# Attention heads in the order 3, 7, 0, 4, 1, 5, 2, 6, with the q copies split by column half

## The chip, the cores and the metric

The kernel runs on one core of a Trainium2 chip. The metric is the device time of one launch in microseconds (us), lower is better. One launch works through a batch of 8 graphs, one after the other, with the same program for each.

## The reference

Input is `x` (8 x 1024 nodes x 256 features), an adjacency `adj` (8 x 1024 x 1024) and a node mask. Four pre-normed residual layers follow each other; the second is the one that the change touches:

```python
h = jnp.maximum(_layernorm(x, axis=-1), 0.0)
x = x + _L1_gnn_ref(h, adj, adj, Wq, bq, Wk, bk, Wv, bv, Wo, bo, 1024)
# in _L1_gnn_ref: 8 heads of 32 features
q, k, v = (proj(Wq, bq), proj(Wk, bk), proj(Wv, bv))
scores = jnp.einsum('bhqd,bhkd->bhqk', q, k) * SCALE
scores = scores * (adj_matrix + bond_matrix)[:, None, :, :]
attn = jax.nn.softmax(scores, axis=-1)
ctx = jnp.einsum('bhqk,bhkd->bhqd', attn, v)        # heads side by side: 256 features
return jnp.einsum('bse,fe->bsf', ctx, Wo) + bo
```

The order in which heads are taken changes nothing in the result as long as the rows of `Wo` follow it.

## The kernel before

Every engine has its own hand-written instruction stream; counters (semaphores, one `Signal` per step) order them. A batch is a chain of stages: graph layer 0, attention (layer 1), hypergraph convolution (layer 2), dense graph attention (layer 3). Nothing of the next batch's matmul work overlaps the attention of this one, so a delay at the start of the attention moves all that is behind it.

**How q and k reach the score matmuls.** Projection gives q and k transposed, features on the partitions: 2 groups of 4 heads, 32 partitions a head. Each value is split into a rounded part and the rest: `khi`, `klo`, `qhi`, `qlo` (128 partitions x 2 groups x 1024 nodes, 8 KB a partition each). A score matmul contracts over 128 partitions at once, in which the four products hi·hi, hi·lo, lo·hi, lo·lo of one head are stacked: `kS[:, head]` holds khi, khi, klo, klo and `qS[:, head]` holds qhi, qlo, qhi, qlo in its four blocks of 32 partitions. A head has a place j (0 to 3) in its group of four (`HPG`). Places 0, 1 and 2 are brought into the stacks by DMA from the SP queue: for each place 4 copies for kS and 4 for qS, each 32 partitions x 2 groups x 1024 columns (256 KB). These are 24 copies a batch. Place 3 (heads 3 and 7) is stacked by TensorE with `pick` matrices (L940) and moved by ScalarE (L865). `K_DONE` is the count of `lo_s` at which all of k is split; SP starts the kS copies there, all three places, and then the qS copies.

**The attention loop.** A unit u is one head of one tile of 128 queries, 64 units a batch (`UNITS`), 8 heads for each of 8 tiles. For unit u: `scores(u)` on TensorE (2 matmuls, L1056, into PSUM banks 0 to 3 in turn); the mask, scale and row maximum on VectorE (L684, writes `Z`); the exponential on ScalarE (L882); `transposes(u)` on TensorE (8, L1076, three PSUM banks in turn); `evacuate(u)` copies them to `PT`, one half by ScalarE (L874), one by VectorE (L645), every fourth unit both by ScalarE; after four units `weighted_values` (L1097). TensorE issues scores of unit u + 2 ahead of the transposes of unit u.

Two things in this order matter. `scores(0)`, `(1)`, `(2)` each wait for one place of qS, since heads 0, 1 and 2 come first, and the whole loop is behind the wait for all of kS:

```python
pe.wait_ge(*kS_in(b, 64 * (HPG - 1)))
...
if u < HPG - 1:
    pe.wait_ge(*qS_in[u](b, 64))
```

And `PT` lies in the same memory as the sources of the copies (region p1: `khi`, `klo`, `qhi`, `qlo` in one layout, 8 slots of `PT` of 4 KB a partition in the other): slots 0 to 3 lie over khi and klo, slots 4 to 7 over qhi and qlo. Before, the waits of TensorE cover this, as every copy has landed before the evacuation of unit 0, 1 or 2 can begin.

`keep_warm` are matmuls without use (L962) that keep TensorE busy.

Of the kernel before, what the change touches and what calls it, by code (L numbers as in the profile page):

```python
# [5 lines left out]
F32 = mybir.dt.float32  # L6
# [8 lines left out]
LOWEST = -3.0e38  # L15
TINY = 1.2e-38


# [11 lines left out]
def build_program(nc, x_in, adj_in, mask_in, wqkT0, wv0, w1attn, bq1, bk1, bv1, bo1,  # L30
# [4 lines left out]
    NH = N // HALF  # L35
# [9 lines left out]
    PTS = 8  # L45
    ZS = 3
    SCORE_SCALE = 2.0 * float(HD) ** -0.5
    W_SCALE = 1.0 / float(D) ** 0.5

    ctx = ExitStack()  # L50
    with ctx:
# [131 lines left out]
        x_free = signal("x_free", 1)  # L183
        kS_in = signal("kS_in", 64 * (HPG - 1))
        qS_in = [signal(f"qS_in{j}", 64) for j in range(HPG - 1)]
        last_ps = signal("last_ps", 2 * GROUPS * NH)
# [149 lines left out]
        KQ = ((0, 0, 0), (0, 0, 1), (0, 1, 0), (1, 0, 0), (1, 0, 1), (0, 1, 1), (1, 1, 0), (1, 1, 1))  # L336
        K_DONE = 5

# [15 lines left out]
        def half(n):  # L354
            return slice(n * HALF, (n + 1) * HALF)

        def heads_of(t):
# [6 lines left out]
        def _(sp):  # L364
# [32 lines left out]
            def batch(b, last):  # L397


                sp.wait_ge(*lo_s(b, K_DONE))  # L400
                stand(sp, waited_sp)
                for dst, parts in ((kS, (khi, khi, klo, klo)), (qS, (qhi, qlo, qhi, qlo))):
                    if dst is qS:
                        sp.wait_ge(*lo_s(b, 2 * GROUPS * NH))
                        stand(sp, waited_sp)
                    for j in range(HPG - 1):
                        done = kS_in if dst is kS else qS_in[j]
                        for r, src in enumerate(parts):
                            to = dst[HD * r:HD * r + HD].rearrange("p (g j) n -> p g j n", j=HPG)[:, :, j]
                            sp.dma_start(to.bitcast(F32), src[HD * j:HD * j + HD].bitcast(F32)).then_inc(done.sem, 16)  # L410

                sp.wait_ge(*pv_ps(b, NT * GROUPS))
                stand(sp, waited_sp)
                if not last:
                    load_w1()
                sp.dma_start(W1h[:], w1T.rearrange("(t p) d -> p t d", p=P)).then_inc(w2_in.sem, 16)
                sp.dma_start(W2g[:], w2T.rearrange("(t p) d -> p t d", p=P)).then_inc(w2_in.sem, 16)
                sp.dma_start(b1B[:], b1.partition_broadcast(P)).then_inc(w2_in.sem, 16)
                sp.dma_start(wB[:], adj_in[bass.ds(b, 1)][0, 0].partition_broadcast(P)).then_inc(wB_in.sem, 16)
                sp.wait_ge(*a3_ps(b, NT))  # L420
                stand(sp, waited_sp)
                for i, w in enumerate(w3attn):
                    sp.dma_start(W3v[:, :, 0:D] if i == 2 else W3[:, i], w.rearrange("(t p) d -> p t d", p=P)).then_inc(w3_in.sem, 16)
                if not last:
                    load_x(b + 1)
                    load_adj(b + 1)
                sp.wait_ge(*x3s(b, NT))
                stand(sp, waited_sp)
                sp.dma_start(out[bass.ds(b, 1)].rearrange("o (t p) d -> p (o t) d", p=P), x[:]).then_inc(out_s.sem, 16)
                sp.wait_ge(*out_s(b, 16))  # L430
                sp.sem_inc(x_free.sem, 1)
# [68 lines left out]
        def _(dve):  # L500
# [58 lines left out]
            def batch(b, last):  # L559
# [78 lines left out]
                def evacuate(u):  # L638
                    if evacuates_both(u):
                        return  # L640
                    bank = turn_bank((u, 1))
                    dve.wait_ge(*T_ps(b, 2 * u + 2))
                    if u >= PTS:
                        dve.wait_ge(*pv_ps(b, (u - PTS) // HPG + 1))
                    dve.tensor_copy(PT[:, u % PTS, NT // 2:NT], heads_of(ps[:, bank])).then_inc(PT_dve.sem, 1)  # L645
# [188 lines left out]
        def _(act):  # L834
# [8 lines left out]
            def batch(b, last):  # L843
# [22 lines left out]

                def evacuate(u):
                    for half_of_u in range(1 + evacuates_both(u)):
                        bank = turn_bank((u, half_of_u))
# [66 lines left out]
        def _(pe):  # L936
# [36 lines left out]
            def batch(b):  # L973
# [75 lines left out]
                def scores(u):  # L1049
                    t, hd = u // HEADS, u % HEADS  # L1050
                    if u >= 2:
                        pe.wait_ge(*zs(b, u - 1))
                    if u < HPG - 1:
                        pe.wait_ge(*qS_in[u](b, 64))
                    for s in range(NH):
# [31 lines left out]
                def weighted_values(g, part):  # L1087
# [6 lines left out]
                    for kt in range(sum(PARTS[:part]), sum(PARTS[:part + 1])):  # L1094
                        for j in range(HPG):
                            hd = HPG * (g % GROUPS) + j
                            mm = pe.matmul(ps[HD * j:HD * j + HD, 7, 0:P],  # L1097
# [9 lines left out]

                pe.wait_ge(*lo_s(b, 2 * GROUPS * NH))
                pe.wait_ge(*lasts(b, 2 * GROUPS * NH - 3))
                keep_warm(0, 1)  # L1110
                pe.wait_ge(*kS_in(b, 64 * (HPG - 1)))
                pe.wait_ge(*vs(b, NT))
                pe.wait_ge(*lasts(b, 2 * GROUPS * NH))
                scores(0)
                keep_warm(turn_bank((0, 1)), 1)
                scores(1)
                keep_warm(turn_bank((0, 1)), 1)
                for u in range(STEPS):
# [173 lines left out]
```

## Time and profile before

| | |
|---|---|
| Time of 3 runs | 3476.94 us median (3474.12 to 3478.45) |
| Profiled execution, span | 3470.2 us |
| Median of the runs over that span | 6.7 us more, at the launch and the end |
| TensorE busy | 3228.3 us (93%) |
| VectorE, ScalarE, GpSimd busy | 60%, 43%, 17% |
| Time from one batch to the next | about 430 us |

The profile is of one execution. Busy time of TensorE counts a matmul in flight as busy, so its 93% does not mean that it computes at its peak. The chain of waits follows what ended last; its part "SPq" is time in which the SP queue was issuing DMAs that the rest stood behind.

### The profile page before, as it was taken

To read this page: it belongs to the slowest core of one execution; us is meant where nothing else is said; L and a number is where in the kernel's file an instruction comes from. 1 tells how busy PE (TensorE), PEld (TensorE's weight loads), DVE (VectorE), ACT (ScalarE), POOL (GpSimd) and SP (SyncE) were. 2 spreads that over 40 slices of the span, in tenths; PEclk is the share of its full clock that TensorE was granted. 3 is DMA by queue.
4 is the path that set the end of the run, shared out by engine and by line. 5 is a ranking of instruction groups with operands and counts; after the bars stand their busy time and mean duration, and the time that the engine had idled before them with its cause. 6 is when DMAs were issued, how large, how long until landed. Compare 5 with 4: busy or idle time off the path is not lost.

```text
span 3470.2 us, 64880 instructions
## 1 busy us (share of the span) xinstructions
PE 3228.3 (93%) x23756; PEld 2474.6 (71%) x23756; DVE 2083.0 (60%) x5009; ACT 1481.4 (43%) x2785; POOL 591.7 (17%) x400
## 2 busy tenths in 40 slices
PE   6899998999989999899998999989999899998999
PEld 5577785777857778577785777767777677676776
DVE  2587425974358743587436874368743686437863
ACT  1483215832158321583315823158221682226722
POOL 0123001230012300123001230012300122001320
PEclk9999999999999999999999999999999999999999
DMA  3300103001030110300103001030010300112000
GB/s 106 74 2 31 70 14 74 2 31 71 13 74 2 31 71 13 74 2 31 71 14 74 2 31 71 14 74 2 31 70 19 69 2 31 70 42 46 23 10 13
DMA packets 67430, 135.69 MB, mean 39 GB/s; under 512 B 6928, under 2 KB 42256, under 8 KB 67088
## 3 DMA queue, kind: packets, MB, share of 16 engines
q1 hardware_dynamic: 67088, 131.13, 13.6%
q8 instruction: 214, 3.51, 0.4%
q14 instruction: 128, 1.05, 0.1%
HBM read 72.39 MB, written 8.39 MB: 23 GB/s over the span
## 4 chain that ended last, share of the span: by engine, by line
PE 69%; DVE 12%; issue 6%; SPq 6%; ACT 4%; DMA 2%; POOL 0%; DVEq 0%; ACTq 0%; POOLq 0%
PE ps L940 31%; PE ps L1076 14%; PE ps L1140 10%; PE ps L1097 6%; SPq L410 6%; PE ps L1056 6%; DVE junk L723 4%; PE ps L986 2%; DMA qS<-qlo 1%; ACT Z L882 1%; DVE stats L523 1%; DVE h2T L741 1%; PE ps L1084 1%; ACT h L840 1%; DVE hT L557 1%
## 5 line engine op out<-in xcount | busy, mean ns | idle before, releaser
L684 DVE CUSTOM_DVE_ANT_0 Z<-ps,adjN 128x1024 f32<-128x1024 f32 x512 | 620.7, 1212 | 151.0 <-PE ps L1056 139.2
L882 ACT ACTIVATE Z<-Z,nm 128x1024 f32<-128x1024 f32 x512 | 587.5, 1148 | 140.4 <-DVE nm L689 139.0
L1076 PE MATMUL ps<-ident,Z 128*128 128x128 f32 x4096 | 559.7, 280 | 29.7 <-ACT Z L882 27.8
L1076 PEld LDWEIGHTS ps<-ident,Z 128*128 128x128 f32 x4096 | 455.2, 142 | 142.1 <-issue 102.6
L1056 PE MATMUL ps<-kS,qS 128*128 128x512 f32 x1024 | 377.1, 451 | 87.5 <-DMA qS<-qlo 87.2
L874 ACT ACTIVATE PT<-ps 128x512 f32<-128x512 f32 x640 | 364.6, 591 | 30.2 <-PE ps L1076 30.2
L1097 PE MATMUL ps<-PT,v 128*32 128x128 f32 x8192 | 300.0, 277 | 3.7 <-ACT Rs L879 3.7
L1097 PEld LDWEIGHTS ps<-PT,v 128*32 128x32 f32 x8192 | 203.3, 109 | 134.5 <-issue 134.5
L645 DVE COPY PT<-ps 128x512 f32<-128x512 f32 x384 | 264.1, 688 | 9.7 <-PE ps L1076 6.1
L467 POOL TENSOR_SCALAR rs<-sm 128x128 f32<-128x128 f32 x128 | 68.5, 535 | 1133.9 <-DVE sm L649 1133.9
L1056 PEld LDWEIGHTS ps<-kS,qS 128*128 128x128 f32 x1024 | 163.4, 196 | 112.8 <-DMA qS<-qlo 92.8
L476 POOL TENSOR_SCALAR H<-adjN 128x1024 fp32r<-128x1024 f32 x64 | 233.5, 3648 | 0.0
L453 POOL TENSOR_SCALAR ve<-mv 128x4 f32<-128x4 f32 x80 | 15.6, 195 | 1224.8 <-DVE mv L528 1223.3
L940 PE MATMUL ps<-v,P 128*128 128x257 f32 x1024 | 223.6, 379 | 0.0
L940 PE MATMUL ps<-mh,adjT 128*128 128x256 f32 x1024 | 222.3, 379 | 0.0
L940 PE MATMUL ps<-hT,t3T 128*128 128x512 f32 x512 | 221.0, 592 | 0.0
L940 PEld LDWEIGHTS ps<-v,P 128*128 128x128 f32 x1024 | 193.8, 189 | 31.9 <-issue 3.8
L940 PEld LDWEIGHTS ps<-mh,adjT 128*128 128x128 f32 x1024 | 194.6, 190 | 26.5
L940 PEld LDWEIGHTS ps<-hT,t3T 128*128 128x128 f32 x512 | 97.2, 190 | 119.1 <-issue 118.6
L580 DVE CUSTOM_DVE_ANT_0 E<-ps,G 128x256 f32<-128x256 f32 x64 | 27.2, 425 | 246.5 <-PE ps L940 246.5
L940 PE MATMUL ps<-W,hT 128*128 128x256 f32 x768 | 174.3, 380 | 0.0
L940 PE MATMUL ps<-W2g,h2T 128*128 128x256 f32 x512 | 134.2, 425 | 36.7 <-issue 31.7
(160 smaller groups left out, 5462.4 us busy)
## 6 DMA issues: line engine op xcount, KB each, us to landing
adjN<-adj_in SPq DMA_DIRECT2D x8, 4096.0 KB, 16.3
kS<-khi SPq DMA_DIRECT2D x48, 256.0 KB, 5.0
kS<-klo SPq DMA_DIRECT2D x48, 256.0 KB, 5.0
qS<-qhi SPq DMA_DIRECT2D x48, 256.0 KB, 5.3
qS<-qlo SPq DMA_DIRECT2D x48, 256.0 KB, 5.3
xn<-x_in SPq DMA_DIRECT2D x8, 1024.0 KB, 6.3
out<-x SPq DMA_DIRECT2D x8, 1024.0 KB, 4.8
W1h<-w1T SPq DMA_DIRECT2D x9, 512.0 KB, 5.3
```

What stands on the lines that cost most here:

```text
L410: sp.dma_start(to.bitcast(F32), src[HD * j:HD * j + HD].bitcast(F32)).then_inc(done.sem, 16)
L476: pool.tensor_scalar(H[:, t], adjN[:, t], 0.0, 0.0, ALU.is_equal, ALU.is_equal).then_inc(Hs.sem, 1)
L645: dve.tensor_copy(PT[:, u % PTS, NT // 2:NT], heads_of(ps[:, bank])).then_inc(PT_dve.sem, 1)
L684: dve.tensor_tensor_reduce(Z[:, u % ZS], ps[:, 2 * (u % 2):2 * (u % 2) + 2].rearrange("p a n -> p (a n)"), adjN[:, u // HEADS], SCORE_SCAL ...
L723: dve.scalar_tensor_tensor(junk[:], H[:, t].bitcast(F32), 1.0, wB[:], ALU.mult, ALU.mult, accum_out=dn[:, 0, t:t + 1]).then_inc(dns.sem, 1)
L874: act.activation(PT[:, u % PTS, first:first + NT // 2], heads_of(ps[:, bank]), ACT.Copy).then_inc(PT_act.sem, 1)
L882: act.activation(Z[:, u % ZS], Z[:, u % ZS], ACT.Exp, bias=nm[:, u:u + 1], accum_out=sm[:, u:u + 1]).then_inc(exps.sem, 1)
L940: mm = pe.matmul(dst, lhsT, rhs, start=(i == 0), stop=(i == len(pairs) - 1))
L1056: mm = pe.matmul(ps[:, 2 * (u % 2) + s], qS[:, hd, rows(t)], kS[:, hd, half(s)], start=True, stop=True)
L1076: mm = pe.transpose(ps[:, turn_bank((u, s)), rows(a)], Z[:, u % ZS, rows(NT // 2 * s + a)], ident[:])
L1097: mm = pe.matmul(ps[HD * j:HD * j + HD, 7, 0:P], v[:, kt, HD * hd:HD * hd + HD], PT[:, (HPG * g + j) % PTS, kt], start=(kt == 0), stop=(kt ...
L1140: mm = pe.matmul(dst(n, i), lhs(n, j, i), rhs(n, j, i), start=(j == 0 and i == 0), stop=(j == NT - 1 and i == 0))
```

## The change

`ORDER = (3, 7, 0, 4, 1, 5, 2, 6)`: for each query tile, units take the heads in this order, so the two that TensorE stacks come first, then both heads of place 0, of place 1, of place 2. The values of a group and the rows of `Wo` follow the order. Each place of kS has a wait of its own, each place and column half of qS too. SP issues: kS place 0, qS place 0 first half of the columns, the same of place 1, of place 2, and then the second halves of qS of all three. The q copies are so 24 of 32 x 2 x 512 (128 KB) where they were 12 of 256 KB; the kS copies are the same 12. The first half of the columns is the first four query tiles. The evacuations of unit 0 and of unit 4, on ScalarE and VectorE, wait explicitly for the copies whose sources `PT` overwrites. The three `keep_warm` and two waits ahead of the loop are gone.

```diff
+HEAD_ORDER = (3, 7, 0, 4, 1, 5, 2, 6)
...
-        K_DONE = 5
+        K_DONE, Q0_DONE = 5, 6
...
+        def stacked(engine, b, u):
+
+            if u == 0:
+                for j in range(HPG - 1):
+                    engine.wait_ge(*kS_in[j](b, 64))
+            if u == PTS // 2:
+                for s in range(NH):
+                    for j in range(HPG - 1):
+                        engine.wait_ge(*qS_in[s][j](b, 64))
...
+                def stack(dst, parts, j, cols, done):
+
+                    for r, src in enumerate(parts):
+                        to = dst[HD * r:HD * r + HD].rearrange("p (g j) n -> p g j n", j=HPG)[:, :, j, cols]
+                        sp.dma_start(to.bitcast(F32), src[HD * j:HD * j + HD, :, cols].bitcast(F32)).then_inc(done.sem, 16)
+
                 sp.wait_ge(*lo_s(b, K_DONE))
                 stand(sp, waited_sp)
-                for dst, parts in ((kS, (khi, khi, klo, klo)), (qS, (qhi, qlo, qhi, qlo))):
-                    if dst is qS:
-                        sp.wait_ge(*lo_s(b, 2 * GROUPS * NH))
+                for j in range(HPG - 1):
+                    stack(kS, (khi, khi, klo, klo), j, slice(0, N), kS_in[j])
+                    if j == 0:
+                        sp.wait_ge(*lo_s(b, Q0_DONE))
                         stand(sp, waited_sp)
-                    for j in range(HPG - 1):
-                        done = kS_in if dst is kS else qS_in[j]
-                        for r, src in enumerate(parts):
-                            to = dst[HD * r:HD * r + HD].rearrange("p (g j) n -> p g j n", j=HPG)[:, :, j]
-                            sp.dma_start(to.bitcast(F32), src[HD * j:HD * j + HD].bitcast(F32)).then_inc(done.sem, 16)
+                    stack(qS, (qhi, qlo, qhi, qlo), j, half(0), qS_in[0][j])
+                sp.wait_ge(*lo_s(b, 2 * GROUPS * NH))
+                stand(sp, waited_sp)
+                for j in range(HPG - 1):
+                    stack(qS, (qhi, qlo, qhi, qlo), j, half(1), qS_in[1][j])
...
+                    stacked(dve, b, u)
                     dve.wait_ge(*T_ps(b, 2 * u + 2))
...
                 def evacuate(u):
+                    stacked(act, b, u)
...
                 def scores(u):
-                    t, hd = u // HEADS, u % HEADS
+                    t, hd = u // HEADS, ORDER[u % HEADS]
                     if u >= 2:
                         pe.wait_ge(*zs(b, u - 1))
-                    if u < HPG - 1:
-                        pe.wait_ge(*qS_in[u](b, 64))
+                    if hd < HPG - 1:
+                        if t == 0:
+                            pe.wait_ge(*kS_in[hd](b, 64))
+                        if t % TPH == 0:
+                            pe.wait_ge(*qS_in[t // TPH][hd](b, 64))
...
-                pe.wait_ge(*lo_s(b, 2 * GROUPS * NH))
-                pe.wait_ge(*lasts(b, 2 * GROUPS * NH - 3))
-                keep_warm(0, 1)
-                pe.wait_ge(*kS_in(b, 64 * (HPG - 1)))
                 pe.wait_ge(*vs(b, NT))
                 pe.wait_ge(*lasts(b, 2 * GROUPS * NH))
                 scores(0)
-                keep_warm(turn_bank((0, 1)), 1)
                 scores(1)
-                keep_warm(turn_bank((0, 1)), 1)
```

On TensorE, at the start of the attention loop, this stood before (the names in the brackets are the signals waited for; L962 is a `keep_warm`):

```order
L940 MATMUL ps<-qlo,pick 128x512
L962 MATMUL ps<-adjT,ident 128x512 [waits lasts,lo_s]
L1111 ISA
L1054 ISA [waits lasts,vs,kS_in]
L1056 MATMUL ps<-kS,qS 128x512 [waits qS_in0]
L1056 MATMUL ps<-kS,qS 128x512
L962 MATMUL ps<-adjT,ident 128x512
L1056 MATMUL ps<-kS,qS 128x512 [waits qS_in1]
```

and the same place of the changed kernel, up to the scores of the third unit, is this (all its line numbers are higher; L1081 are the scores, L1101 the transposes):

```order
L962 MATMUL ps<-qlo,pick 128x512
L1081 MATMUL ps<-kS,qS 128x512 [waits lasts,vs]
L1081 MATMUL ps<-kS,qS 128x512 x3
L1097 ISA
L1101 MATMUL ps<-ident,Z 128x128 [waits exps]
L1101 MATMUL ps<-ident,Z 128x128 x7
L1077 REGISTER_ALU [waits zs]
L1081 MATMUL ps<-kS,qS 128x512 [waits qS_in00,kS_in0]
```

The first two units' scores have moved ahead of every wait for a copy; the third unit (head 0) is the first that waits for one, and only for place 0.

On the SP queue, in each batch, this stood before for kS (its last rows) and qS (its first rows):

```order
L410 DMA kS<-khi 32x2x1024 x2
L410 DMA kS<-klo 32x2x1024 x2
L404 REGISTER_ALU
L410 DMA qS<-qhi 32x2x1024 [waits lo_s]
L410 DMA qS<-qlo 32x2x1024
```

and now, from the first kS copy of place 0 to the first kS copies of place 1:

```order
L417 DMA kS<-khi 32x2x1024 [waits lo_s]
L417 DMA kS<-khi 32x2x1024
L417 DMA kS<-klo 32x2x1024 x2
L424 REGISTER_ALU
L417 DMA qS<-qhi 32x2x512 [waits lo_s]
L417 DMA qS<-qlo 32x2x512
L417 DMA qS<-qhi 32x2x512
L417 DMA qS<-qlo 32x2x512
L417 DMA kS<-khi 32x2x1024 x2
```

Four half-width q copies have moved in between the kS copies of place 0 and those of place 1; behind the last of place 2 stand the 12 of the second column half.

On ScalarE, in the first five units, the changed kernel has these rows at the evacuations of unit 0 and (after the dots) unit 4, where before only `T_ps` was waited for:

```order
L904 ACTIVATE Z,sm<-Z,nm 128x1024 [waits nms]
L364 REGISTER_ALU
L892 ISA [waits kS_in2,kS_in1,kS_in0]
L896 ACTIVATE PT<-ps 128x512 [waits T_ps]
...
L904 ACTIVATE Z,sm<-Z,nm 128x1024 [waits nms]
L892 REGISTER_ALU [waits qS_in10,qS_in11,qS_in02,qS_in12,qS_in01,qS_in00]
L896 ACTIVATE PT<-ps 128x512 [waits T_ps]
```

The two new waits stand on ScalarE (and the same on VectorE) ahead of the first write to `PT` slot 0 and slot 4; the exponentials of unit 2 and later stand behind the first, those of unit 6 and later behind the second.

## Rows read from the trace of the kernel before

**Rows 1.** Page: span, busy time of each engine, chain that ended last.
```profile
span 3470.2 us, 64880 instructions
PE 3228.3 (93%) x23756; PEld 2474.6 (71%) x23756; DVE 2083.0 (60%) x5009; ACT 1481.4 (43%) x2785; POOL 591.7 (17%) x400
PE 69%; DVE 12%; issue 6%; SPq 6%; ACT 4%; DMA 2%; POOL 0%; DVEq 0%; ACTq 0%; POOLq 0%
```

**Rows 2.** Waits of PE: who waited for whom, us in total, times, longest.
```profile
PE ps L1056 <- DMA qS<-qlo: 87.2, 24, 7.5
```

**Rows 3.** Timeline of the first batch, 107 to 142: start, length, what, idle before.
```profile
107.93 0.75 DVE L633 SCALAR_TENSOR_TENSOR klo<-ps,bk1c,khi 128x512 fp32r<-128x512 f32 x1 [0.96 <-ACT khi L860]
109.64 0.75 DVE L633 SCALAR_TENSOR_TENSOR qlo<-ps,bq1c,qhi 128x512 fp32r<-128x512 f32 x1 [0.97 <-ACT qhi L860]
121.60 2.06 ACT L865 ACTIVATE qS<-ps 128x512 fp32r<-128x512 f32 x4 [3.26 <-PE ps L940]
122.57 0.39 PE L940 MATMUL ps<-qlo,pick 128*128 128x512 f32 x1
131.28 1.22 PE L1056 MATMUL ps<-kS,qS 128*128 128x512 f32 x2 [7.46 <-DMA qS<-qlo]
136.12 0.73 PE L1056 MATMUL ps<-kS,qS 128*128 128x512 f32 x2 [1.91 <-DMA qS<-qlo]
140.96 1.62 PE L1056 MATMUL ps<-kS,qS 128*128 128x512 f32 x4 [2.37 <-DMA qS<-qlo]
```

**Rows 4.** Chain that ended last, in order of time, 108 to 141: start, length, what.
```profile
108.77 0.73 SPq L410
109.55 0.58 SPq L410
110.18 0.67 SPq L410
110.90 1.36 SPq L410
112.30 1.25 SPq L410
...
134.43 0.60 SPq L410
135.07 5.75 DMA qS<-qlo
```

**Rows 5.** Tile kS: its copies' time to landing over all batches.
```profile
DMA to landing us min/median/max: 3.2/5.0/5.1
```

**Rows 6.** Timeline, first batch, the loop's first units from the third exponential on.
```profile
143.37 1.15 ACT L882 ACTIVATE Z<-Z,nm 128x1024 f32<-128x1024 f32 x1 [3.15 <-DVE nm L689]
143.90 1.21 DVE L684 CUSTOM_DVE_ANT_0 Z<-ps,adjN 128x1024 f32<-128x1024 f32 x1
144.52 0.58 ACT L874 ACTIVATE PT<-ps 128x512 f32<-128x512 f32 x1
150.54 0.59 ACT L874 ACTIVATE PT<-ps 128x512 f32<-128x512 f32 x1
```

**Rows 7.** The same two places of the eighth batch.
```profile
3142.11 1.18 PE L1056 MATMUL ps<-kS,qS 128*128 128x512 f32 x4 [0.20 <-DMA qS<-qlo]
3151.55 0.59 ACT L874 ACTIVATE PT<-ps 128x512 f32<-128x512 f32 x1
```

**Rows 8.** Stretches: length, busy of PE, PEld, DVE, ACT, POOL, PEclk, DMA share, GB/s.
```profile
124.00:128.00 4.00, 0.00 (x0) 0.00 (x0) 0.00 (x0) 0.00 (x0) 0.00 (x0) 0.98 1.00 218
128.00:132.00 4.00, 0.72 (x2) 0.62 (x3) 0.00 (x0) 0.00 (x0) 0.00 (x0) 0.50 1.03 213
132.00:136.00 4.00, 2.21 (x4) 0.54 (x2) 1.39 (x3) 1.24 (x2) 0.00 (x0) 0.67 1.03 223
140.00:144.00 4.00, 3.04 (x13) 2.66 (x13) 2.05 (x5) 0.85 (x2) 0.00 (x0) 0.68 0.00 0
18.00:22.00 4.00, 4.00 (x11) 3.19 (x10) 0.75 (x2) 0.00 (x0) 0.00 (x0) 1.00 1.02 418
```

**Rows 9.** Page, DMA issues: tile, count, KB each, median us to landing.
```profile
adjN<-adj_in SPq DMA_DIRECT2D x8, 4096.0 KB, 16.3
qS<-qlo SPq DMA_DIRECT2D x48, 256.0 KB, 5.3
xn<-x_in SPq DMA_DIRECT2D x8, 1024.0 KB, 6.3
```

More of the change, by code:

```diff
@@ L46, in build_program @@
     ZS = 3
+    ORDER = HEAD_ORDER
     SCORE_SCALE = 2.0 * float(HD) ** -0.5
@@ L183, in build_program @@
         x_free = signal("x_free", 1)
-        kS_in = signal("kS_in", 64 * (HPG - 1))
-        qS_in = [signal(f"qS_in{j}", 64) for j in range(HPG - 1)]
+        kS_in = [signal(f"kS_in{j}", 64) for j in range(HPG - 1)]
+        qS_in = [[signal(f"qS_in{s}{j}", 64) for j in range(HPG - 1)] for s in range(NH)]
         last_ps = signal("last_ps", 2 * GROUPS * NH)
@@ L1095, in weighted_values @@
                         for j in range(HPG):
-                            hd = HPG * (g % GROUPS) + j
+                            hd = ORDER[HPG * (g % GROUPS) + j]
                             mm = pe.matmul(ps[HD * j:HD * j + HD, 7, 0:P],
@@ L1274 @@
         "x_in": x, "adj_in": adj, "mask_in": columns(nodemask), "wqkT0": T(L0_gnn_Wqk), "wv0": L0_gnn_Wv,
-        "wq1": T(L1_gnn_Wq), "wk1": T(L1_gnn_Wk), "wv1": T(L1_gnn_Wv), "wo1": T(L1_gnn_Wo),
+        "wq1": T(L1_gnn_Wq), "wk1": T(L1_gnn_Wk), "wv1": T(L1_gnn_Wv),
+        "wo1": T(L1_gnn_Wo).reshape(len(HEAD_ORDER), -1, x.shape[-1])[list(HEAD_ORDER)].reshape(x.shape[-1], -1),
         "bq1": columns(L1_gnn_bq), "bk1": columns(L1_gnn_bk), "bv1": L1_gnn_bv, "bo1": L1_gnn_bo,
```

## The prediction

> **What bounds the kernel now.** The page first: TensorE is busy 93% of the span, and in the chain that ended last it has 69%. That would say that only matmul work counts, but the same chain gives 6% to "SPq", a queue that only issues DMAs [rows 1]. A DMA queue in the chain means that in some stretch everything stands behind copies. The waits of TensorE say which: the score matmuls waited 87.2 us for copies of qS, 24 times, which is three times a batch [rows 2]. That is 10.9 us a batch.
>
> The timeline of the first batch shows them. The last product with `pick` starts at 122.57, and from there TensorE has nothing but one keep-warm until 131.28; scores of unit 0, 1 and 2 start at 131.28, 136.12 and 140.96, each released by a copy of qS [rows 3]. The steps between are 4.84 us, four copies. So what bounds this stretch is the stream of 24 copies. The chain shows its parts one behind the other from 108.77, and the last one, issued at 135.07, lands 5.75 later, at 140.82 [rows 4]. After unit 2 the loop runs freely: exponential of unit 2 at 143.37, evacuation of unit 4 at 150.54 [rows 6].
>
> What limits the stream? The DMA engines are busy for 1.00 to 1.03 of the time at 213 to 223 GB/s [rows 8]. The fastest landing of a copy is 3.2 us [rows 5], so the first one, issued at 108.77, is in at about 112.0. From there to 140.82 the other 23 land, one each 1.253 us. The queue's own issue takes only 0.73, 0.58 and 0.67 for the first three; the fourth takes 1.36 and ends at 112.26, just after the first landed, and then they take about 1.25 [rows 4]. I read this as at most four copies in flight, each new one let in when one lands: an effect of the transfer rate, not of the issue.
>
> **What moves.** Four things.
>
> *Units 0 and 1 first.* Heads 3 and 7 need only ScalarE's last move into qS: four of them from 121.60, two of the products behind the first start later, so they end at about 123.7 [rows 3]. Their scores can run at 123.8 and 124.5 where they ran at 131.28 and 136.12. This alone gains nothing if something later stays where it is, so the question is what is late next.
>
> *Copies, in the new order.* The kS copies are unchanged, 12 of 1.25. The bytes of q are the same too, but in 24 copies of half the size. Their price h isn't in this trace. From below: half of a whole one, 0.625, if the rate of bytes is all. From above: 1.25, if a copy costs the same whatever its size. The nearest rows are these. A 4 KB row of `adjN` goes at 418 GB/s over all 128 partitions [rows 8], which is twice the copies' rate with rows of the same 4 KB between 32 partitions and 32 partitions. So the copies' 1.25 is not a cost for each row. `xn`, 1024 rows of 1 KB, 64 for each of 16 DMA engines, lands in 6.3 us [rows 9], so a 1 KB row costs at most 98 ns, where one of our 4 KB rows costs 1.25 / 4 = 313 ns; a straight line between gives 170 ns at 2 KB, four of them 0.68 us. The issue itself is the other bound: 0.58 to 0.73 with a gap of 0.05, 0.71 in the mean [rows 4], and it doesn't hold the first 12 halves back, since whole copies between them leave the queue ahead. I take h = 0.68.
>
> The Trainium skill ("SBUF — State Buffer", section "Door 1: The DMA port swizzle") says that DMA bandwidth depends on how many of 16 ports the partitions reach, and that partitions 0 to 31 reach 8. The trace agrees: 213 against 418 GB/s. By this rule alone h would be 0.625 and the stream would end as before.
>
> *The stream's times.* It is in service from 112.0 − 1.25 = 110.8. kS place 0 lands by 115.8, the halves of q place 0 by 118.5, kS 1 by 123.5, q 1 by 126.2, kS 2 by 131.2, q 2 by 133.9, and the 12 of the second half by 110.8 + 15.0 + 24 × 0.68 = 142.1. The waits for k and first q done (109.64 + 0.75 for the q one) are over before place 0 of kS is issued at about 112.3 [rows 3, 4]. Head 0's scores, at about 127.6 behind the transposes of unit 0, find their copies landed; head 1's (unit 4, about 133) and head 2's (unit 6, about 136) too. No score matmul waits for a copy any more.
>
> *The new waits.* The evacuation of unit 0 waits for all of kS: 131.2. It would otherwise be ready at about 128.7 (scores 123.8, row maximum, exponential, transposes), so ScalarE and VectorE stand for 2.5 us. Behind it on ScalarE is the exponential of unit 2, on VectorE the mask of unit 3; TensorE gets no further than half of unit 1's transposes, as three banks are full. From there the loop runs as now: exponential of unit 2 at 131.9 (behind an evacuation of 0.58), and 150.54 − 143.37 = 7.2 us later [rows 6] the evacuation of unit 4, at 139.1. But this is the second new wait, for all of q: 142.1. So the last landing, not the arithmetic, still sets when unit 4 gets through; with 0.2 for the semaphore, 142.3.
>
> **The sum.** Unit 4's evacuation stands at 150.54 in the first batch, 9.6 behind scores of unit 2; in the eighth it is 151.55 − 142.11, 9.4 [rows 6, 7, 3]. Behind it nothing of the program has changed: same units, same operations, only other columns of v and rows of Wo. Gain a batch: 150.54 − 142.3 = 8.2 us, and 8 batches give 66 us. On the profiled execution 3470.2 − 66 = 3404, and with the 6.7 outside the span 3411. The three keep-warms removed lie in waits and cost or give nothing. Extra waits (3 and 6 on two engines, 12 on TensorE) are passed while the last of them still is pending.
>
> **The clock.** The granted clock is 0.98 at 124 to 128 and 0.50 at 128 to 132, after TensorE stood idle for 4 us; it is 0.68 at 140 to 144, behind another gap [rows 8]. In the changed kernel TensorE has little to do from 124 to 131, so I expect about the same drop to 1.2 GHz at 128 to 135, now with work in it: from 131 to 139 some 5 us of matmul work at full clock. At half clock for 4 us it loses 2 us, and 142.1 − 139.1 leaves 3.0 for that. This cover falls away if the copies end sooner than I say.
>
> **Rivals.**
>
> *A, the halves are dearer than 0.68, yet under 1.0 (0.17).* A copy could pay a fixed part, for instance if the four in flight are the limit and landing has a fixed share: 3.2 − 1.25 = 1.95 of the first copy, and (1.95 + 0.625) / 4 = 0.64; if that share grows to 2.7 under load, h is 0.83. The issue cost of 0.73 points the same way. At 0.83 all q lands at 145.7, the gain is 4.6 a batch, 37 in all: 3440. The Trainium skill ("DMA: Bandwidth & Descriptors", section "Measured (HBM→SBUF, 128 partitions, SWDGE, issued from GpSimd)") has this as a rule: batch DMAs to 1 MiB or more. No row here shows a copy of 128 KB.
>
> *B, a half costs what a whole does (0.06).* Then all q lands at 110.8 + 36 × 1.25 = 155.8, unit 4 stands until then, and each batch loses 5.5: 44 us more, 3521. It decides from h = 1.02, where 24 halves end at 150.3. Against it: 418 GB/s with rows of the same size.
>
> *C, the gain is given back (0.06).* If SP's order or the waits left the loop waiting for the same thing as now, or the half clock lasted through the first units (5 us of work taking 10, twice 4 us with the second stall), 0 to 3 us a batch stay: 3453 to 3477, 3465 in the middle. Against it: before, the same drop at 140 to 144 cost the loop little.
>
> *D, the copies end as before and the stall is made up behind it (0.06).* h = 0.625 or less, evacuation of unit 4 at 141.0 and work laid up by the exponentials ahead, 0.5 more: 10 us a batch, 3397.
>
> *Forecast (0.65):* 3411, its own range 3402 to 3424, h from 0.62 to 0.74.
>
> **How the numbers follow.** I take the likeliest, 3411. From 3398 to 3442 the range holds the forecast, A and part of D, and leaves out B and C. A measurement of this kernel tells about 0.2%, 7 us. Faster by over 0.2% are the forecast, A, D and most of C, 0.90; within 0.2% part of C, 0.03; slower B and a rest, 0.07.
>
> **What the profile after would show.** The waits of TensorE have no or nearly no row of scores behind a copy. Scores start at about 124 in the first batch. ScalarE's and VectorE's idle time has two stretches a batch ahead of `PT`, of 2 to 3 us each, released by copies of kS and of qS. The issues of the halves take 0.6 to 0.7 and their landing some 2.7 us; the last lands at about 142. Share of SPq in the chain stays near 6%, as the stream still is the path up to unit 4. It is wrong if the last landing is after 146, or if ScalarE's first evacuation of unit 4 is not held by a copy at all.

## The result and the profile after

The changed kernel takes 3421.72 us (median of 4 runs, 3418.15 to 3426.04), the kernel before 3477.3 beside it: ratio 0.9846, 95% interval 0.9832 to 0.9860. A gain of 55.6 us, where 66 was forecast, inside the range of 3398 to 3442. The two profiled spans differ by less, 53.8 us. The 6.7 us by which the median of the kernel before lies above its profiled span are not all launch and end: in every other execution of these kernels the time is 1.7 to 3.4 us more than the execution's own span, 1.8 in most. So the profiled execution of the kernel before was probably some 5 us faster than the median.

The page of the changed kernel, to be held against [rows 1]:

```profile
span 3416.4 us, 64985 instructions
PE 3209.0 (94%) x23708; PEld 2475.0 (72%) x23708; DVE 2088.2 (61%) x5009; ACT 1482.4 (43%) x2785; POOL 591.0 (17%) x400
...
PE 70%; DVE 12%; SPq 7%; issue 6%; ACT 4%; DMA 1%; POOL 0%; DVEq 0%; ACTq 0%; POOLq 0%
...
qS<-qhi SPq DMA_DIRECT2D x96, 128.0 KB, 2.9
```

TensorE is busy 19 us less, which says nothing of the gain. "SPq" is still in the chain with 7%: the copies still set the end of something. The waits (who waited for whom, total us, times, longest; TensorE, then ScalarE, then VectorE) say of what:

```profile
PE ps L1101 <- ACT PT L896: 28.5, 17, 3.4
PE ps L1081 <- ACT qS L886: 6.8, 8, 0.8
...
ACT PT L896 <- DMA qS<-qlo: 23.5, 8, 3.5
ACT PT L896 <- DMA kS<-klo: 10.5, 4, 2.7
...
DVE PT L666 <- DMA qS<-qlo: 21.9, 8, 3.4
```

The 87.2 us of score matmuls behind copies [rows 2] are gone; the scores (L1081) wait for nothing but ScalarE's last move. The copies are waited for by the evacuations now: once a batch for qS, 2.9 us on ScalarE, and TensorE's transposes wait behind that. The wait for kS is named in four batches only, but the evacuation of unit 0 comes 22.6 to 22.8 us behind the first copy's issue in all eight. The first batch in the timeline, beside [rows 3, 6]; all of it lies 0.33 later here, as the first copy is issued at 109.10 and not at 108.77:

```profile
124.14 1.15 PE L1081 MATMUL ps<-kS,qS 128*128 128x512 f32 x4 [0.84 <-ACT qS L886]
128.63 1.91 PE L1081 MATMUL ps<-kS,qS 128*128 128x512 f32 x4
131.92 0.60 ACT L896 ACTIVATE PT<-ps 128x512 f32<-128x512 f32 x1 [2.68 <-DMA kS<-klo]
142.41 0.60 ACT L896 ACTIVATE PT<-ps 128x512 f32<-128x512 f32 x1 [2.86 <-DMA qS<-qlo]
143.06 1.12 PE L1101 MATMUL ps<-ident,Z 128*128 128x128 f32 x4 [2.73 <-ACT PT L896]
146.82 1.97 PE L1101 MATMUL ps<-ident,Z 128*128 128x128 f32 x8
```

Scores of units 0 and 1 start at 124.14 instead of 131.28 and 136.12. The evacuation of unit 4 starts at 142.41, with a wait for the last q copy directly ahead of it. And the chain that ended last, same stretch, shows that copy and what the halves cost the queue, beside [rows 4]:

```profile
137.69 0.60 SPq L417
138.34 0.60 SPq L417
138.98 3.25 DMA qS<-qlo
142.41 0.60 ACT PT L896
```

A half is issued each 0.64 us (0.60 and the gap), and the last lands at 138.98 + 3.25 = 142.23. In each of the eight batches the evacuation of unit 4 starts 0.18 us behind the last landing.

So far this is the forecast. What is missing stands behind unit 4. I took two distances in each of the eight batches: from the first copy's issue to the evacuation of unit 4, and from there to the exponential of unit 10 (the fifth `PT` row of ScalarE, adjacent ones taken as one, and the eleventh exponential behind the first kS issue). Sums over eight batches, in us:

| | to evacuation of unit 4 | on to exponential of unit 10 | both | span |
|---|---|---|---|---|
| before | 333.1 | 82.5 | 415.6 | 3470.2 |
| after | 267.1 | 92.8 | 359.9 | 3416.4 |

The first fell by 66.0, the whole forecast. The second rose by 10.2, although its program is the same. The rest of the program makes up the difference to the spans: the attention from unit 10 on is 1.2 shorter, and the stretch from its last exponential to the next batch's first copy, or to the end, 2.8 longer. Before, the second distance was 10.31 or 10.32 in every batch; after, it was 12.78, 12.31, 11.59, 10.30, 11.55, 10.30, 11.47 and 12.47. The stretch of 10 us behind unit 4's evacuation, by batch (columns as in [rows 8]), for batches 1, 3, 4, 5 and 6:

```profile
143.10:153.10 10.00, 10.00 (x99) 7.61 (x100) 6.10 (x15) 6.89 (x14) 3.28 (x2) 0.69 0.00 0
...
990.50:1000.50 10.00, 9.63 (x104) 7.52 (x105) 7.20 (x15) 7.66 (x15) 3.94 (x2) 0.83 0.00 0
1414.10:1424.10 10.00, 9.75 (x126) 7.44 (x128) 8.34 (x18) 7.95 (x16) 4.15 (x2) 1.00 0.01 2
1834.40:1844.40 10.00, 10.00 (x110) 7.97 (x109) 7.10 (x17) 7.43 (x14) 4.15 (x2) 0.83 0.00 0
2257.20:2267.20 10.00, 9.75 (x122) 7.44 (x126) 8.33 (x18) 7.84 (x16) 4.15 (x2) 1.00 0.01 2
```

Read the granted clock, the third number from the end. Where it is 1.00 (batches 4 and 6) the distance is the old 10.3; where it is 0.83 it is 11.5, where it is 0.69 it is 12.8. TensorE got 99 matmuls into the 10 us of batch 1 and 126 into those of batch 4, and it was busy throughout in both. This is the theory to test: the new gap on TensorE ahead of the transposes that wait for unit 4's evacuation (2.73 us in the first batch, 2.4 to 3.4 in all) is itself part of the first distance, but behind it the clock is at the lower of its two levels, 1.2 GHz, for part of the time in six of eight batches, and then TensorE is the engine that everything waits for. The length of the gap doesn't tell which batches are hit: in batch 5 it was 2.40 us and the clock fell, in batch 6 it was 2.53 and the clock stayed.

### The profile page after: what moved, and what is told of

Its sections match the earlier page's. It is cut to its first block, busy times and chain, and to the rows that moved or that the text cites. A ratio compares the mean times of both kernels' runs of the same rounds, so it can differ in the third digit from the quotient of the medians.

```text
span 3416.4 us, 64985 instructions
## 1 busy us (share of the span) xinstructions
PE 3209.0 (94%) x23708; PEld 2475.0 (72%) x23708; DVE 2088.2 (61%) x5009; ACT 1482.4 (43%) x2785; POOL 591.0 (17%) x400
## 4 chain that ended last, share of the span: by engine, by line
PE 70%; DVE 12%; SPq 7%; issue 6%; ACT 4%; DMA 1%; POOL 0%; DVEq 0%; ACTq 0%; POOLq 0%
PE ps L962 31%; PE ps L1101 14%; PE ps L1159 10%; SPq L417 7%; PE ps L1122 6%; PE ps L1081 5%; DVE junk L744 4%; PE ps L1008 2%; DVE h2T L762 1%; DVE stats L543 1%; PE ps L1109 1%; ACT h L861 1%; DVE hT L577 1%; DVE h L769 1%; PE ps L992 1%
## 5 line engine op out<-in xcount | busy, mean ns | idle before, releaser
L1101 PE MATMUL ps<-ident,Z 128*128 128x128 f32 x4096 | 570.2, 283 | 73.1 <-ACT Z L904 43.6
L1101 PEld LDWEIGHTS ps<-ident,Z 128*128 128x128 f32 x4096 | 459.9, 143 | 185.9 <-issue 97.8
L1081 PE MATMUL ps<-kS,qS 128*128 128x512 f32 x1024 | 374.3, 450 | 6.8 <-ACT qS L886 6.8
L962 PE MATMUL ps<-v,P 128*128 128x257 f32 x1024 | 223.6, 380 | 0.0
L962 PE MATMUL ps<-mh,adjT 128*128 128x256 f32 x1024 | 222.3, 380 | 0.0
L962 PE MATMUL ps<-hT,t3T 128*128 128x512 f32 x512 | 221.0, 593 | 0.0
L962 PEld LDWEIGHTS ps<-v,P 128*128 128x128 f32 x1024 | 194.2, 190 | 31.5 <-issue 3.8
L962 PEld LDWEIGHTS ps<-mh,adjT 128*128 128x128 f32 x1024 | 195.0, 190 | 26.0
L962 PEld LDWEIGHTS ps<-hT,t3T 128*128 128x128 f32 x512 | 97.5, 190 | 118.9 <-issue 118.4
L1081 PEld LDWEIGHTS ps<-kS,qS 128*128 128x128 f32 x1024 | 165.9, 198 | 14.7 <-issue 10.0
L962 PE MATMUL ps<-W,hT 128*128 128x256 f32 x768 | 174.3, 380 | 0.0
L962 PE MATMUL ps<-W2g,h2T 128*128 128x256 f32 x512 | 135.4, 428 | 38.9 <-issue 34.4
```

Source lines behind the costliest of these rows:

```text
L962: mm = pe.matmul(dst, lhsT, rhs, start=(i == 0), stop=(i == len(pairs) - 1))
L1081: mm = pe.matmul(ps[:, 2 * (u % 2) + s], qS[:, hd, rows(t)], kS[:, hd, half(s)], start=True, stop=True)
L1101: mm = pe.transpose(ps[:, turn_bank((u, s)), rows(a)], Z[:, u % ZS, rows(NT // 2 * s + a)], ident[:])
```

## The experiments

Every kernel was timed beside the kernel before on the same chip; ratios are to that, with 95% intervals. "The changed kernel" stands for the one above.

**The changed kernel again.**

> The changed kernel itself once more, so that the next two have it beside them on the same chip: 3422 within 5 us.

Measured 3421.11 us, ratio 0.9842 (0.9829 to 0.9856). In this profile seven of eight batches had the longer distance behind unit 4 (11.5 to 12.7, and one of 10.30), 92.0 in all. Which batches are hit changes from one execution to another; the sum hardly does.

**Heads in the old order, copies in the new one.**

```diff
-HEAD_ORDER = (3, 7, 0, 4, 1, 5, 2, 6)
+HEAD_ORDER = (0, 1, 2, 3, 4, 5, 6, 7)
```

> The changed kernel with the heads in the order 0 to 7 again; the split copies, their order and all waits stay. Theory (the landing of the last q copy sets when unit 4 gets through, wherever heads start): scores of unit 1 wait for place 1 until about 127, those of unit 2 for place 2 until about 134; exponential of unit 2 at about 136, and unit 4's evacuation 7.2 behind it, at 143.4, where the changed kernel has 142.4. So 1 us a batch dearer, 8 us in all, and up to 16 more if the longer gap halves TensorE's granted clock for the following units: 3430 to 3446. Rival (the order is what brought the gain): the gain goes, 3465 to 3477.

Measured 3423.35 us, ratio 0.9848 (0.9832 to 0.9864): the same as the changed kernel. The waits of TensorE and the timeline of the first batch:

```profile
PE ps L1081 <- DMA qS<-qlo: 47.2, 16, 4.8
```
```profile
134.00 2.04 PE L1081 MATMUL ps<-kS,qS 128*128 128x512 f32 x4 [4.81 <-DMA qS<-qlo]
...
144.20 0.59 ACT L896 ACTIVATE PT<-ps 128x512 f32<-128x512 f32 x1
```

The scores wait for copies again, half as long as before the change, unit 2 until 134.00. Unit 4 is evacuated at 144.20, 1.8 us later than in the changed kernel. But no copy holds it, so TensorE has no such gap there, and the granted clock of the next 8 us is 1.00:

```profile
144.00:148.00 4.00, 3.32 (x42) 2.67 (x43) 3.72 (x9) 3.01 (x8) 0.00 (x0) 1.00 0.00 0
148.00:152.00 4.00, 4.00 (x59) 2.88 (x58) 2.92 (x9) 4.00 (x8) 2.31 (x2) 1.00 0.00 0
```

The distance behind unit 4 is 10.3 in all batches. What the order saves ahead of unit 4, 13 us in eight batches (280.3 here, 267.1 there), the clock takes back to 10 behind it (82.5 here, 92.8 there). My expectation was 8 to 24 us slower, 8 for the later start and up to 16 for the clock, and it missed: I gave the changed kernel no loss of its own.

This run shows one thing more. Its copies are those of the changed kernel, yet the last lands 32.2 us behind the first issue in the mean of eight batches, and 33.2 in the changed kernel. In the changed kernel a load of 16 KB of instructions runs on the same DMA engines in the window 138 to 141:

```profile
q8 instruction: 1, 0.02, 2.5%
```

The stretches from 140 to 142, first of the changed kernel, then of this run (PEclk, DMA share and GB/s are the last three numbers):

```profile
140.00:141.00 1.00, 0.33 (x4) 0.09 (x1) 0.00 (x0) 0.00 (x0) 0.00 (x0) 1.00 0.19 47
141.00:142.00 1.00, 0.00 (x0) 0.00 (x0) 0.00 (x0) 0.00 (x0) 0.00 (x0) 1.00 0.58 133
...
140.00:141.00 1.00, 0.90 (x8) 0.63 (x7) 0.97 (x4) 0.77 (x4) 0.00 (x0) 1.00 0.87 197
141.00:142.00 1.00, 0.93 (x7) 0.49 (x5) 1.00 (x3) 1.00 (x1) 0.15 (x1) 1.00 0.03 6
```

In the changed kernel the DMA engines are nearly idle for a while and then move the last copy; here they have moved it by about 141. The load starts 29.1 to 30.4 us behind the first issue in all eight batches of the changed kernel, and so in its second profile (29.1 to 30.6); here it starts 32.4 or more behind it, when the last copy has landed. So the last copy of the changed kernel comes 1.0 us later than its stream alone would bring it, 8 us in eight batches. That the load is what holds it is read from the times, as no run moved the load alone.

**Matmuls without use in the gap, 12 of them.**

```diff
                     for s in range(2):
+                        if (u, s) == (PTS // 2 + 1, 1):
+                            keep_warm(7, 12)
                         wait_bank((u, s))
```

> The changed kernel with 12 matmuls without use (512 columns, PSUM bank 7, 2.6 us at full clock) on TensorE in its gap ahead of unit 5's second half of transposes, where it waits for the evacuation of unit 4. Theory (the gap of 2.7 us there halves the granted clock for the next 3 to 7 us in six of eight batches, and this takes back 2 us in each): the clock stays at 1.00 behind the gap and the time falls by 8 to 16 us, to 3406 to 3414. Rival (the loss behind unit 4 is of VectorE and ScalarE, whose order of work the stall has upset): no change, 3422, or slower by the matmuls' tail, 3425.

Measured 3457.77 us, ratio 0.9944 (0.9927 to 0.9960), 36 us slower. The size was wrong, as the timeline shows:

```profile
139.70 10.47 PE L984 MATMUL ps<-adjT,ident 128*128 128x512 f32 x24
142.49 0.60 ACT L896 ACTIVATE PT<-ps 128x512 f32<-128x512 f32 x1 [3.40 <-DMA qS<-qlo]
...
150.00 0.60 PE L1103 MATMUL ps<-ident,Z 128*128 128x128 f32 x4
```

A `keep_warm` is fp32 and is recorded as two matmuls; 12 take 10.47 us, 0.87 each. They ended 7 us after the evacuation that they should have filled the time to. The granted clock behind them is 1.00 in all batches, but what that is worth is lost in the 7 us, so the time decides nothing on the theory.

**The same with 3 of them.**

```diff
-                            keep_warm(7, 12)
+                            keep_warm(7, 3)
```

> The run with 12 matmuls without use took 3457.8: each lasts 0.87 us, not 0.22, so they ran on for 7 us past the gap. Now 3 of them, 2.6 us for a gap of 2.7. Theory (the gap ahead of unit 4's evacuation halves the granted clock of what follows, 2 us in six of eight batches): clock 1.00 behind it in all batches, 8 to 16 us below the changed kernel's 3422: 3406 to 3414. Rival (the loss has nothing to do with the clock): 3422.

Measured 3401.28 us, ratio 0.9789 (0.9775 to 0.9802); by the ratios 20 us below the changed kernel. Timeline, and the stretch behind unit 4 in batch 1 (the other seven have 1.00 too):

```profile
141.42 2.74 PE L984 MATMUL ps<-adjT,ident 128*128 128x512 f32 x6
143.47 0.60 ACT L896 ACTIVATE PT<-ps 128x512 f32<-128x512 f32 x1 [2.67 <-DMA qS<-qlo]
```
```profile
144.10:154.10 10.00, 9.75 (x119) 7.42 (x122) 8.34 (x19) 7.72 (x16) 4.14 (x2) 1.00 0.01 2
```

The wait for the last copy is about the same, the evacuation starts no earlier (267.8 us in all behind the first issues, 267.1 there), the kernel has more work; only the gap is filled, and the clock stays up. The distance behind unit 4 is 10.3 in all eight batches, 82.4 in all, 10.4 less. This shows the theory.

The profiled spans differ by 16.4. The rest lies late in the batches: from the last exponential of the attention to the next batch's first copy, or to the end, it is 2000.6 us here and 2008.6 in the changed kernel, and 2001.1 in the run with 12. There too the clock differs. In batch 2, from 226.8 us behind the first copy on, first the changed kernel, then this one:

```profile
759.70:763.10 3.40, 3.40 (x10) 2.65 (x9) 1.01 (x3) 0.42 (x1) 0.00 (x0) 0.50 0.00 0
...
758.60:762.00 3.40, 3.40 (x19) 2.96 (x18) 2.33 (x6) 0.83 (x2) 0.00 (x0) 1.00 0.00 0
```

The program there is the same and TensorE is busy throughout in both. Why matmuls in the gap at unit 4 should raise the clock some 195 us later no run shows. So of the 20 us, 10 are explained by the gap that was filled.

**q copies whole, between the kS copies.**

```diff
...
-                        sp.wait_ge(*lo_s(b, Q0_DONE))
+                        sp.wait_ge(*lo_s(b, 2 * GROUPS * NH))
                         stand(sp, waited_sp)
-                    stack(qS, (qhi, qlo, qhi, qlo), j, half(0), qS_in[0][j])
-                sp.wait_ge(*lo_s(b, 2 * GROUPS * NH))
-                stand(sp, waited_sp)
-                for j in range(HPG - 1):
-                    stack(qS, (qhi, qlo, qhi, qlo), j, half(1), qS_in[1][j])
+                    stack(qS, (qhi, qlo, qhi, qlo), j, slice(0, N), qS_in[0][j])
...
```

The waits for q on TensorE and at unit 4 are reduced to match, one for each place.

> The changed kernel with the q copies whole again (12 of 256 KB instead of 24 of 128 KB), between the kS copies of the same place. Theory (the last landing sets the evacuation of unit 4): the last lands at about 141.2, all of kS at about 136.2 in place of 131.9; the first evacuation waits for that, and unit 4's comes 7.8 later, at 144.1 against 142.4. As in the run with the natural order there is then no second gap and no half clock behind it, which gives 1.7 a batch back: 3420 to 3426. If the clock plays no part: 3436. If the 24 halves themselves cost what was missing: 3414 or less.

Measured 3425.51 us, ratio 0.9858 (0.9842 to 0.9873), as expected with the clock's part. The first evacuation now waits until 27.8 to 28.1 us behind the first issue (22.8 in the changed kernel) for all of kS, and TensorE waits 6.1 us behind it in place of 2.7 later:

```profile
PE ps L1096 <- ACT PT L891: 47.9, 9, 6.1
```

Unit 4 comes at 284.6 in all batches, 2.2 later in each than with halves, and behind it runs at 10.3. So in this mixed order the halves do serve: they let kS in earlier, 17.5 us in eight batches. They lose 10.3 of it again behind the gap.

**Without the second column half.**

```diff
...
-                sp.wait_ge(*lo_s(b, 2 * GROUPS * NH))
-                stand(sp, waited_sp)
-                for j in range(HPG - 1):
-                    stack(qS, (qhi, qlo, qhi, qlo), j, half(1), qS_in[1][j])
...
-                        mm = pe.matmul(ps[:, 2 * (u % 2) + s], qS[:, hd, rows(t)], kS[:, hd, half(s)], start=True, stop=True)
+                        mm = pe.matmul(ps[:, 2 * (u % 2) + s], qS[:, hd, rows(t % TPH)], kS[:, hd, half(s)], start=True, stop=True)
```

> The changed kernel without the 12 copies of the second column half and without the waits for them. What is left out: query tiles 4 to 7 take the q of tiles 0 to 3 (the same matmuls on other columns), so the output of half the rows is that of other rows. Theory: the evacuation of unit 4 is no longer held, comes at 139.7 in place of 142.4, and TensorE has no gap behind which the clock falls: 2.8 + 1.7 a batch, 36 us below the changed kernel, 3386. Rival (the loop makes up the stall by itself, since exponentials were ahead): 3415 to 3422.

Measured 3376.95 us, ratio 0.9717 (0.9704 to 0.9731), 9 us less than the 3386 that I expected; the profiled span is 3379.6, 36.8 below the changed kernel's. The evacuation of unit 4 in the first batch, behind a first issue at 109.8:

```profile
140.08 0.59 ACT L891 ACTIVATE PT<-ps 128x512 f32<-128x512 f32 x1
```

It is 30.3 behind the first issue in place of 33.3, waits for nothing, and what follows takes 10.3. 24.2 us in eight batches come from the first distance, 10.2 from the second. The second column half and the wait for it at unit 4 thus cost the changed kernel 34 us, more than half of what the change brought. Where the other 10 us between the medians come from isn't shown; the profiled execution was the slowest of the five.

**New head order, copies as before the change.**

```diff
...
                 for j in range(HPG - 1):
                     stack(kS, (khi, khi, klo, klo), j, slice(0, N), kS_in[j])
-                    if j == 0:
-                        sp.wait_ge(*lo_s(b, Q0_DONE))
-                        stand(sp, waited_sp)
-                    stack(qS, (qhi, qlo, qhi, qlo), j, half(0), qS_in[0][j])
                 sp.wait_ge(*lo_s(b, 2 * GROUPS * NH))
                 stand(sp, waited_sp)
                 for j in range(HPG - 1):
-                    stack(qS, (qhi, qlo, qhi, qlo), j, half(1), qS_in[1][j])
+                    stack(qS, (qhi, qlo, qhi, qlo), j, slice(0, N), qS_in[0][j])
...
```

> The new head order and the separate waits, with the copies as before the change: all of kS, then qS whole, 24 copies. Theory (the copy stream's end sets unit 4, and head order and copy order stand in for one another): q of place 0 lands at 131.3, place 1 at 136.3, place 2 at 141.2; scores of units 2 and 4 wait for the first two, the first evacuation for nothing, unit 4's for the last, 141.4 to 143; no more than 1.5 us a batch from the changed kernel: 3410 to 3434. Rival (the gain is that of the split and mixed copies): close to before, 3460 to 3477.

Measured 3411.66 us, ratio 0.9823 (0.9809 to 0.9837), so at least as fast as the changed kernel; the two intervals just overlap. TensorE's waits for copies, one of them in batch 2, and the 10 us behind unit 4's evacuation in batches 1 and 4:

```profile
PE ps L1076 <- DMA qS<-qlo: 24.7, 14, 1.9
...
562.21 0.70 PE L1076 MATMUL ps<-kS,qS 128*128 128x512 f32 x2 [1.81 <-DMA qS<-qlo]
```
```profile
142.30:152.30 10.00, 9.75 (x121) 7.43 (x121) 8.73 (x19) 7.68 (x16) 4.15 (x2) 1.00 0.01 2
...
1407.60:1417.60 10.00, 9.75 (x112) 7.54 (x112) 7.69 (x19) 7.22 (x14) 3.87 (x2) 0.92 0.00 0
```

Unit 4's evacuation comes at 268.5 in all, 1.4 more than in the changed kernel, and the distance behind it is 86.8 in place of 92.8. The granted clock there is 1.00 in six batches, where the distance is 10.3 to 10.7, and 0.92 in the fourth and the eighth, where it is 11.8. This order of copies meets the slow clock less often. It was also not the last landing itself that released unit 4's evacuation, as I had expected: the last copy landed 31.8 us behind the first issue in the mean, and unit 4 came 1.3 to 2.1 later. In five batches TensorE waited with the scores of unit 6 for that copy, as in the row at 562.21, and unit 4's transposes stand behind them; in batches 1, 3 and 6 it had no such wait.

**Only the new waits.** Heads 0 to 7 and the copies as before: the last two edits together.

> The fourth corner of the square: heads in the order 0 to 7, copies as before the change, only the separate waits of the new kernel (and no keep-warm). Theory (either the head order or the copies' order brings the gain, the waits by themselves nothing): scores of unit 2 at 141.2 as before, 3470 to 3485. Rival (the waits that used to stand ahead of the loop cost time of their own): below 3460.

Measured 3476.66 us, ratio 1.0003 (0.9994 to 1.0012). TensorE waits for each of the three places again:

```profile
PE ps L1076 <- DMA qS<-qlo: 109.4, 24, 8.2
```

It is 22 us more than in [rows 2] at the same time of the kernel: the `keep_warm` matmuls, which this kernel lacks, had lain in that stretch. The two between the scores took 1.91 and 1.02 us in the first batch of the kernel before, which would be 23 in eight. This closes the square:

| | copies as before | copies mixed and halved |
|---|---|---|
| heads 0 to 7 | 3476.66, ratio 1.0003 | 3423.35, ratio 0.9848 |
| heads 3, 7, 0, 4, 1, 5, 2, 6 | 3411.66, ratio 0.9823 | 3421.72, ratio 0.9846 |

Each half of the change brings the gain alone, and both together bring no more. With both, the last landing holds unit 4, and the clock takes 10 us behind it. With only the copies changed, unit 2's scores wait for their copy until 24.9 us behind the first issue, and unit 4 comes at 35.0, when the last copy has landed 2.6 to 3.0 us before. With only the heads changed, the last landing is earlier, 31.8, and TensorE's scores of unit 6 wait for it or come just behind it.

**Start the stream earlier.** New head order; kS copies by column half, the first half issued as soon as the first half of k is split; then the second; q whole.

```diff
...
-                sp.wait_ge(*lo_s(b, K_DONE))
-                stand(sp, waited_sp)
-                for j in range(HPG - 1):
-                    stack(kS, (khi, khi, klo, klo), j, slice(0, N), kS_in[j])
-                    if j == 0:
-                        sp.wait_ge(*lo_s(b, Q0_DONE))
-                        stand(sp, waited_sp)
-                    stack(qS, (qhi, qlo, qhi, qlo), j, half(0), qS_in[0][j])
+                for s in range(NH):
+                    sp.wait_ge(*lo_s(b, (GROUPS, K_DONE)[s]))
+                    stand(sp, waited_sp)
+                    for j in range(HPG - 1):
+                        stack(kS, (khi, khi, klo, klo), j, half(s), kS_in[s][j])
                 sp.wait_ge(*lo_s(b, 2 * GROUPS * NH))
                 stand(sp, waited_sp)
                 for j in range(HPG - 1):
-                    stack(qS, (qhi, qlo, qhi, qlo), j, half(1), qS_in[1][j])
+                    stack(qS, (qhi, qlo, qhi, qlo), j, slice(0, N), qS_in[0][j])
...
```

> The new head order with the kS copies split by column half, the first half issued when the first half of k is ready, 6.5 us before now, then the second, then q whole. Theory (the last landing of the copy stream sets unit 4, so starting the stream earlier is worth its full time until the arithmetic takes over): the last q copy lands at about 134.8, unit 4's evacuation is held by no copy and comes at about 137 in place of 142.4, and no gap halves the clock behind it: 5.3 to 6.8 us a batch, 3368 to 3380. Rival (half copies at 0.64 us each from the queue eat what the early start gives, or they disturb the projections): 3400 or more.

Measured 3373.5 us, ratio 0.9703 (0.9690 to 0.9716): 103 us below the kernel before, 48 below the changed one, and the fastest of all with the full computation. Its page's chain and the timeline of the first batch:

```profile
PE 74%; DVE 14%; issue 6%; ACT 4%; DMA 0%; POOL 0%; DVEq 0%; SPq 0%; ACTq 0%; POOLq 0%
```
```profile
102.57 1.36 SPq L417 DMA_DIRECT2D kS<-khi  x2
...
130.57 1.22 SPq L417 DMA_DIRECT2D qS<-qlo  x1
...
139.50 0.59 ACT L893 ACTIVATE PT<-ps 128x512 f32<-128x512 f32 x1
```

SPq has left the chain. The last copy is issued at 130.57 and lands at 135.7 (I had expected 134.8), and unit 4's evacuation at 139.50 waits for no copy. That is 2.5 later than I expected, so the time fell into my range for another reason than I gave. The span is 42.1 below the changed kernel's: 22.6 of it, 2.8 a batch, because unit 4 comes earlier (counted from the last split of q), 10.2 behind unit 4, and 9 between the attention and the next batch's last split of q, which nothing here explains. Around the first transposes the clock is low:

```profile
128.00:132.00 4.00, 4.00 (x21) 3.50 (x19) 1.39 (x3) 1.69 (x4) 0.00 (x0) 0.58 1.01 226
```

TensorE is busy throughout these 4 us at a granted clock of 0.58, work that full speed would do in some 2.3. That would account for most of the 2.5, but no run filled this earlier gap, so it is only argued. The distance behind unit 4 is 10.3 in all batches.

## Why the forecast held, and where it was off

- **Which wait bounds the start: right.** The 87.2 us of scores behind copies are gone, and the waits moved to the evacuations of units 0 and 4, as said: 2.68 us in the first batch for kS (said: 2.5), 2.86 for qS (said: 3.0).
- **The price of a half copy: a little too high, and the landing right by luck.** 0.64 us were measured where I took 0.68 from a line between two row lengths. It is the queue's issue, 0.60 and 0.04, against 0.625 that the bytes would take: the DMA engines are busy for 0.88 of the time from 136 to 138, where they were busy for 1.00 to 1.03 with whole copies [rows 8]. The last landing was 142.23, to be compared with 142.1 and the shift of 0.33. But 24 halves at 0.64 end 1.0 us earlier than at 0.68, as they do in the run with the heads in the old order, and in the changed kernel the last copy is 1.0 late, beside a load of instructions that I hadn't thought of. The two errors cancel. Rivals A and B fall with the 0.64, and D with the last landing, which is later than before and not as before.
- **The sum to unit 4: right, with that luck in it.** 66.0 us in eight batches, forecast 66. Without the late last copies it would have been some 8 more, since the arithmetic alone gets to unit 4 sooner still (30.4 behind the first issue in the mean, without the second half of q).
- **"Behind it nothing of the program has changed": the step that failed.** The program hasn't, the clock has. I priced the clock's drop only for the gap at 124 to 131, and covered it with the 3.0 us of waiting ahead of the last landing. That cover held: the granted clock is 0.50 from 130 to 134 and 0.59 from 134 to 136, and unit 4 still waits for the copy. But the same 3 us of waiting are a second gap on TensorE, and behind that one there is no cover. I put its cost at nothing; it was 10.2 us. The rows to see it by were there: before the change the granted clock was 0.68 at 140 to 144, behind a gap of 2.37 us [rows 3, 8]. I noted it and set it aside, as it cost the loop little at that place. 66.0 − 10.2 = 55.8. That the medians differ by 55.6 is close to it in part by chance, as the profiled spans differ by 53.8. Rival C had the mechanism with its second stall in it, at 0.06 and as an alternative to the gain and not as a term of it.
- **What I didn't ask** was whether the two halves of the change add up. They don't; each alone brings as much as both. The new head order alone may even be a little faster (0.9823 against 0.9846, intervals that just overlap); by the profiles 6.0 us of that lie behind unit 4, where the clock is lower with both.

## What to carry to other kernels

When waits are moved, look for the one that ends last and ask what it does to TensorE: here gaps of 2.4 to 3.4 us, behind which matmuls set the pace, cost 10 of the 66 us through the clock. Where two edits both shorten the same wait, measure each alone; one may be enough, and the next gain is in moving what the wait ends with, here by starting the copies when half of their source was ready. Filling the known gap with matmuls that nobody needs took 20 us off here, 10 of them directly behind the gap, since they were sized by a row of the trace; four times as many cost 36. And when a forecast hits, check its terms one by one: here two errors of 8 us each had cancelled.

## What the runs showed of the hardware

- The granted clock fell behind a gap on TensorE of 2.4 to 3.4 us in six of eight batches of one execution and in seven of another, and in none when 2.7 us of matmuls stood in it.
- Copies from 32 partitions to 32 partitions ran at 213 to 223 GB/s as 256 KB [rows 8] and at 204 GB/s as 128 KB (136 to 138 of the changed kernel); at 128 KB the queue's issue of 0.60 us and its gap of 0.04 have become the limit.
- In all sixteen batches of the two profiles of the changed kernel a load of 16 KB of instructions, among the last copies of 128 KB, goes with a last landing 1 us later than in the run where the load starts behind them.
- In the last run the first pair of half kS copies took 1.36 us to issue and the later ones 1.24, so its 36 copies, 24 halves and 12 whole ones, left the queue in 29.2 us, where the 24 whole ones of the kernel before had taken 27.4.
